# Attention with the softmax scale in the keys and the maximum written negated

## What is computed

```python
softmax_scale = QHD ** (-0.5) * m * m          # QHD = 128, m = 0.1*log(128) + 1
q = (_rmsnorm(x @ wq_a.T, q_a_ln_w) @ wq_b.T).reshape(B, S, H, QHD)
ckv, k_pe = split(x @ wkv_a.T)                 # 32 latent + 64 rotary columns
kv = (_rmsnorm(ckv, kv_a_ln_w) @ wkv_b.T).reshape(B, S, H, NOPE + VD)
...
scores = jnp.einsum('bqhd,bkhd->bhqk', q_full, k_full) * softmax_scale
scores = jnp.where(causal[None, None], scores, jnp.finfo(scores.dtype).min)
attn = jax.nn.softmax(scores, axis=-1)
out = jnp.einsum('bhqk,bkhd->bqhd', attn, v).reshape(B, S, H * VD)
return out @ wo.T
```

## Time and profile before

| what | value |
|---|---|
| time, median of 3 runs | 1586.24 us (1585.55 to 1586.72) |
| the profiled execution: its time, its span | 1587.04 us, 1585.2 us |
| busy over the span: PE, PEld, DVE, ACT, POOL | 89%, 72%, 47%, 35%, 39% |
| mean granted clock of TensorE | 0.958 |
| span of 224 to 857 us (attention): PE, DVE, ACT, POOL busy | 594.88, 411.66, 339.38, 271.01 us |
| the same for 857 to 1500 us (second attention and experts) | 605.04, 219.71, 146.62, 297.94 us |

### The profile page before, as it was taken

One profiled execution on the slowest core, in us unless ns is written; L12 is line 12 of the kernel. 1 busy time (PEld: TensorE's weight loads), 2 busy tenths in 40 slices (PEclk: granted clock), 3 DMA queues, 4 the chain that ended last, 5 costly groups with the idle time before them and its releaser, 6 DMA issues. The chain is left out here.

```text
span 1585.2 us, 25823 instructions
## 1 busy us (share of the span) xinstructions
PE 1404.6 (89%) x8210; PEld 1143.0 (72%) x8211; DVE 752.0 (47%) x1723; ACT 560.1 (35%) x1743; POOL 622.0 (39%) x521
## 2 busy tenths in 40 slices
PE   3999789999999999999996685999999999999950
PEld 0566467777777777777763485999999999999940
DVE  5221466666666666666665674222222222222227
ACT  0232245555555555555553243112111112112114
POOL 0000234444444444444444366534446254471035
PEclk9899989999999999999998897999999999999985
DMA  8032200000000000000003775545656455564337
GB/s 274 0 107 87 100 14 1 14 14 13 13 14 13 13 13 13 13 13 13 14 21 134 291 266 186 190 144 177 211 175 236 141 186 187 183 231 139 106 112 253
DMA packets 66558, 171.50 MB, mean 108 GB/s; under 512 B 6000, under 2 KB 14592, under 8 KB 66192
## 3 DMA queue, kind: packets, MB, share of 16 engines
q0 software_dynamic: 25712, 97.94, 18.5%
q1 hardware_dynamic: 35040, 62.39, 11.8%
q10 hardware_dynamic: 5760, 10.57, 1.9%
HBM read 125.27 MB, written 45.61 MB: 108 GB/s over the span
## 5 line engine op out<-in xcount | busy, mean ns | idle before, releaser
L1593 PE MATMUL bank<-expert_weights,rows_t 128*128 x1872 | 358.7, 347 | 10.6 <-DVE rows_t L1519 10.6
L1593 PEld LDWEIGHTS bank<-expert_weights,rows_t 128*128 128x128 f32 x1872 | 340.3, 189 | 14.2 <-issue 11.0
L926 POOL TENSOR_TENSOR room<-room 128x1024 f32<-128x1024 f32 (+1 forms) x128 | 187.7, 1466 | 343.2 <-DVE room L837 343.2
L896 ACT ACTIVATE room<-bank,room 128x256 f32<-128x256 f32 (+1 forms) x512 | 207.9, 420 | 131.2 <-DVE room L822 131.0
L696 PE MATMUL bank<-room 96*128 (+2 forms) x1024 | 232.4, 347 | 0.3
L1531 DVE TENSOR_TENSOR x_keep<-x_keep,bank 128x400 f32<-128x400 f32 x78 | 44.5, 571 | 303.2 <-ACT x_keep L1470 301.8
L1025 POOL TENSOR_TENSOR expert_weights<-x_keep,expert_weights 128x1600 fp32r<-128x1600 f32 (+2 forms) x49 | 160.2, 3270 | 49.4 <-DMA expert_weights<-w 49.2
L696 PEld LDWEIGHTS bank<-room 96*128 96x128 f32 x1024 | 156.4, 192 | 28.0 <-issue 1.6
L1616 PE MATMUL bank<-expert_weights,act_t 128*128 x702 | 165.6, 389 | 1.0 <-ACT act_t L1475 1.0
L1616 PEld LDWEIGHTS bank<-expert_weights,act_t 128*128 128x128 f32 x702 | 131.5, 188 | 25.6 <-issue 1.3
L1470 ACT ACTIVATE x_keep<-bank 128x400 f32<-128x400 f32 x78 | 39.3, 504 | 298.0 <-PE bank L1593 298.0
(11 more groups left out here) (241 smaller groups left out, 1912.9 us busy)
## 6 DMA issues: line engine op xcount, KB each, us to landing
x_keep<-w POOLq DMA_DIRECT2D x28, 800.0 KB, 4.9
expert_weights<-w POOLq DMA_DIRECT2D x28, 800.0 KB, 6.4
x_keep<-w POOLq DMA_DIRECT2D x14, 768.0 KB, 5.3
expert_weights<-w POOLq DMA_DIRECT2D x14, 768.0 KB, 6.9
rows_by_expert<-room SPq DMA_DIRECT2D x1, 9984.0 KB, 30.0
x_keep<-rows_by_expert SPq DMA_DIRECT2D x39, 256.0 KB, 3.7
results_by_row<-x_keep ACTq DMA_DIRECT2D x39, 256.0 KB, 5.2
room<-wo SPq DMA_DIRECT2D x16, 512.0 KB, 5.2
```

What stands on the lines that cost most here:

```text
L896: last = sc.activation(Pr[:, m % 4, hh, 0:w], scores_bank(m)[:, w * hh:w * hh + w], ACT.Exp, bias=nb[:, par, hh:hh + 1], scale=SCALE, accu ...
L926: g.tensor_tensor(pr, pr, rs[:, one[1] % 2].unsqueeze(2).broadcast_to([P, 4, w]), ALU.mult).then_inc(normed, 1)
L1593: last = mm(psum(2 * hf + w)[:, 0:HF], xgT[:, par, of_x, P * k:P * k + P], W[:, ds(off + (of_w * SLOT + (k * 2 + w) * FF + hf * HF), HF)], ...
```

## The change

The scale is multiplied into the keys as they leave PSUM. With it in the scores, the exponential takes the default scale, and the bias is the negated maximum, which the reduction writes itself. The multiply by -SCALE, the tile `mx` and the semaphore `maxed` go.

```diff
@@ normalise_latents, VectorE
-                v.tensor_copy(s.KT[0:KC, 512 * g:512 * g + 512], psum(4 + g)[0:KC])
+                v.tensor_scalar(s.KT[0:KC, 512 * g:512 * g + 512], psum(4 + g)[0:KC], SCALE, None, ALU.mult)
@@ attention
-    mx, nb, sm, rs = s.carve(2, 4), s.carve(2, 4), s.carve(2, 4), s.carve(2, 4)
+    nb, sm, rs = s.carve(2, 4), s.carve(2, 4), s.carve(2, 4)
@@ dve_step
             dve.wait_ge(scored, n + 1)
-            v.tensor_reduce(mx[:, par], scores_bank(m)[:, 0:4 * w].rearrange("p (h k) -> p h k", h=4), AX.X,
-                            ALU.max).then_inc(maxed, 1)
-            dve.wait_ge(maxed, n + 1)
-            v.tensor_scalar(nb[:, par], mx[:, par], -SCALE, None, ALU.mult).then_inc(bias_ready, 1)
+            v.tensor_reduce(nb[:, par], scores_bank(m)[:, 0:4 * w].rearrange("p (h k) -> p h k", h=4), AX.X,
+                            ALU.max, negate=True).then_inc(bias_ready, 1)
@@ act_step
                 last = sc.activation(Pr[:, m % 4, hh, 0:w], scores_bank(m)[:, w * hh:w * hh + w], ACT.Exp,
-                                     bias=nb[:, par, hh:hh + 1], scale=SCALE, accum_out=sm[:, par, hh:hh + 1])
+                                     bias=nb[:, par, hh:hh + 1], accum_out=sm[:, par, hh:hh + 1])
```

More of the change, by code:

```diff
@@ L626, in attention @@
     sin = const("sin", "p (k c) -> p k c", k=2)
-    (scored, maxed, bias_ready, expd, summed, normed, chunk_done, roped, q_added, q_turned, q_out, p_turned, p_out,
+    (scored, bias_ready, expd, summed, normed, chunk_done, roped, q_added, q_turned, q_out, p_turned, p_out,
      k1_turned, k1_out, pv_done, o_out, proj_done, proj_used, x_done, q_staged, q_low, v_staged, x_summed,
      stats_done, o_low) = (sem(n) for n in (
-         "scored", "maxed", "bias_ready", "expd", "summed", "normed", "chunk_done", "roped", "q_added", "q_turned",
+         "scored", "bias_ready", "expd", "summed", "normed", "chunk_done", "roped", "q_added", "q_turned",
          "q_out", "p_turned", "p_out", "k1_turned", "k1_out", "pv_done", "o_out", "proj_done", "proj_used",
```

## The result

The changed kernel took 1570.05 us in the median (1566.42 to 1574.43, 4 runs), the kernel before beside it 1585.98: a ratio of 0.990, 95% interval 0.9873 to 0.9927. In two later comparisons it was 0.9923 (0.9908 to 0.9938) and 0.9907 (0.9887 to 0.9928). The gain is 15.9 us in the first, where I had forecast 11.5.

The account below looks back on a forecast made before the run. TensorE was taken to set the pace in the first layer's attention. Six passes at 1.63 us (9.8), plus 1.2, 0.4 and 0.2, less 0.1 for the keys, gave 11.5 us: 1574.7 us, range 1570.5 to 1582.5.

Parts of the forecast that it names:

- step 0: Transposes at step 0 of an entry, waiting 0.61 us for GpSimd's line 926: gain 0.28 us, 0.33 us stays.
- step 4's transposes: Transposes that waited 0.34 us for the normalisation following step 3's maximum: gain 0.28 us per pass.
- steps 5 to 8: Two pairs of waits for GpSimd hidden in weight-load rows, 0.86 us in all: gain 0.76 us per pass.
- the last entry's steps 5 to 8: Same places in the written-out last entry, with the smaller 0.20 us for each step: gain 0.60 us.
- the two long waits: Waits for GpSimd's line 926 at the stage's end, each with one maximum ahead: gain 0.4 us.
- The wait goes; what is late next is TensorE itself. Gain 0.59.: Steps 3 to 5: transposes gain 0.28 us, and the projection's 0.31 us wait for step 4's rope goes.
- Together 1.63 us per pass: Sum for one loop pass over step 0, steps 3 to 5 and steps 5 to 8; times 6 is 9.8 us.
- more arrives: Rival: all waits at these places vanish, 2.4 us per pass, time 1570.2 us; chance 0.05.
- The rope that waits for the maximum's end: Rival: VectorE gains 0.20 us per step instead of 0.28, 1.31 us per pass, time 1576.6 us; chance 0.15.
- Only the own time: Rival: each place gains the instruction's 0.17 us once, 0.82 us per pass, time 1580.6 us; chance 0.15.
- Slower: Rival: line 819's negated maximum costs a second pass over the data, time 1604 us; chance 0.05.
- nothing: Rival: TensorE's waits move to ScalarE's line 882 or its own issue, time stays at 1586 us; chance 0.08.

Follow-up runs that it names:

- step 4 alone: Kernel with scale in the keys and multiply by -1 with its wait at every step except step 4; passes 78.54 us, 0.55 less than with all multiplies.
- the three variants up to the rope that waits: Scale in keys with a separate negating multiply, 1586.79 us; a one-element reduction in its place, 1582.39 us; changed kernel plus a wait before the rope, 1581.48 us.
- steps 5 to 7: Kernel with scale in the keys and multiply by -1 with its wait at every step except 5, 6 and 7; passes 78.30 us, 0.79 less.

## Why the prediction was wrong

What held: the bound and the places. TensorE set the pace, the exposed waits for VectorE's queue were where the change paid, ScalarE's scale and the keys cost nothing, and the negated maximum took the plain one's time. VectorE's queue gained 0.28 us per step (0.88 to 0.60 us), the exponentials 0.20. The terms for step 0 (0.28), for step 4's transposes (0.28), for steps 5 to 8 (0.76 against 0.80) and for the last entry's steps 5 to 8 and the two long waits (1.0 against 1.05) came out.

What failed is the sum for one pass, 1.63 us, where the loop lost 2.20. Times the six passes that is 3.4 of the missing 4.4 us. Two of its steps:

- "The wait goes; what is late next is TensorE itself. Gain 0.59." This term took TensorE's listed wait of 0.31 us as all that the projection could gain. It gained 0.55, because without a wait it starts 0.23 us before the transposes ahead of it end; with step 4 alone freed it was 0.55 as well. Nor is the rope out of the way: the changed kernel's projection still starts 0.13 us behind the rope's end (385.45 + 0.28 = 385.73, then 385.86), as before (389.20, then 389.33), and 0.40 us behind the query transposes, its distance with step 4 alone, where the rope ended 0.23 us ahead. So both limits meet there.
- "Together 1.63 us per pass" has no term for step 12. What TensorE had to gain there, 0.27 us, stood in the weight-load row as 0.40 us put down to issue. I had looked for rows with GpSimd as the releaser.

The rest was not traced to the change. The profiled execution gained 1.8 us by its clock in the drain, which a second profile of the same kernel did not show. Before the first projection 0.2 us were gained, and between the last one and the end 1.6 us were given back; neither is more than these stretches differ among the first six profiles, of the kernel before, the changed one twice, and the three variants up to the rope that waits (267.2 to 269.2 us and 736.8 to 738.5 us).

That the first median fell outside the range was in part chance. The later comparisons gave 1573.05 us, inside it, with a gain of 13.0, and a gain of 12.5 us on another chip. The sum per pass was short by the same 0.57 us every time. Of the 14.1 and 13.9 us that the two profiles gained from the first projection to the last entry's at step 5, some are lost again outside, and how much of that is more than spread is open.

Of the rivals, "more arrives" (1570.2 us, chance 0.05) gave nearly the time, with 2.4 us per pass against 2.20, but by luck in part: it let the whole wait at step 0 go, of which 0.33 us stayed, and had no term for step 12 either. The rope that waits for the maximum's end is refuted by 0.60 us from the start of a 0.68 us maximum to the rope. The Trainium skill (VectorE: DVE Perf Modes, The DRAIN you can't avoid) has the rule behind it, and adds that an instruction that is not held starts earlier; the 0.60 us here agree with that addition. Only the own time: refuted by the 0.79 us of steps 5 to 7. Slower and nothing did not occur. The range was too narrow below: it stopped at 1570.5, above a rival that I had worked out myself. The same kernel before spread over 10 us in 29 runs, so that medians of four runs can differ by some us, which three runs over 1.2 us had not shown me.

## What to carry to other kernels

Where an in-order engine feeds the one that sets the pace, price an instruction that waits for its neighbour by the distance from the neighbour's start to the next independent work, with and without it, and not by its own duration: here 0.28 us per step for an instruction of 0.17, and a wait left in its place kept all of it. Before summing the exposed waits, look at the weight-load rows as well, those put down to issue too, and compare their starts with the end of whatever the semaphore stands for. A listed wait can be too low a figure: where it goes, the next instruction can start before the one ahead has ended (0.55 us gained for 0.31 listed, 0.5 for 0.25). And where a gap is closed, look for a second limit at the same instruction, listed or not, since closing the first alone can gain nothing, as at step 12.

## What the runs showed of the hardware

A wait of VectorE for its own previous instruction kept the next one back by 0.19 us after that had ended; without it the next one started 0.08 us before the end (0.60 us after the start of 0.68). The wait, not the instruction between them, makes the difference of 0.28 us.

A multiply of 128x4 elements with both sides in SBUF took 170 ns, but up to 633 beside GpSimd's additions; a reduction on the same elements took 156 to 158 ns at all 128 places.

In the drain TensorE's granted clock fell to 0.50 (1.2 GHz) in each of the first six profiles, behind a gap of up to 3.8 us, but for 3 to 7 us and not at the same work. Three of the six had another 3 to 4 us at half clock at step 12 of the last entry, behind a wait of 1.4 to 1.6 us that the others had too. The stretch from that entry's projection at step 5 to the one that ends the stage took 60.9 to 65.7 us in the six, which differ little in it. In the steady loop the granted clock was 1.00 in all of them.
